# A transformer block on one core: the attention mask moved into a spare row of keys and queries, and a written-out head and end of the first phase

## The reference, cut to what matters

```python
x = x + L0_xattn(layernorm(x), ctx_768, mask)       # 64 sequences x 128 tokens x 256, 16 heads of 16
x = x + L0_ffn(layernorm(x))                        # top-1 routing to 8 experts, capacity 512 rows each
x = x + L1_xattn(layernorm(x), ctx_768)
x = x + L1_ffn(layernorm(x))                        # six nodes of attention with 8 heads

def L0_xattn(x, context, context_mask, ...):
    q, k, v = x @ Wq, context @ Wk, context @ Wv
    scores = where(context_mask[:, None, None, :], q k^T * 0.25, -finfo.max)
    return softmax(scores) v @ Wo

def L0_ffn(x):
    probs = softmax(x @ w_switch + b_switch); route = probs.argmax(-1)
    slot = route * capacity + running count of the route, or none beyond the capacity
    buf = zeros.at[slot].set(x); y = relu(buf w1 + b1) w2 + b2, per expert
```

## Time and profile before

| what | value |
|---|---|
| time, median of 3 runs | 4100.9 us (4100.56 to 4101.86) |
| the profiled execution's own time | 4101.14 us |
| its span in the trace | 4099.0 us |
| granted TensorE clock, mean | 0.99 |
| busy: PE, DVE, ACT, POOL | 98%, 58%, 64%, 47% of the span |
| first phase | 0 to about 660 us |
| expert phase | about 660 to 899 us |
| second layer | 899 us to the end |

### The profile page before, as it was taken

The page is one execution under the profiler, slowest core; times in us unless marked ns, Lnnn a source line. Parts: engine busy times, 40 slices in busy tenths (PEclk is TensorE's granted clock), DMA queues, the critical chain, the costliest instruction groups (busy, mean ns, idle before and its releaser), DMA issues.

```text
span 4099.0 us, 100758 instructions
## 1 busy us (share of the span) xinstructions
PE 4001.1 (98%) x38276; PEld 3406.3 (83%) x38276; DVE 2391.6 (58%) x6184; ACT 2622.6 (64%) x11786; POOL 1930.3 (47%) x2011
## 2 busy tenths in 40 slices
PE   8999998999999999999999999999999999999997
PEld 6888886668888888888888888888888888888886
DVE  5777772016556566666666666666665565666553
ACT  6888881115666666666666666666666666666664
POOL 5888883013444444444444444444444444444443
PEclk9999999999999999999999999999999999999999
DMA  3232214421000000000000000000000000000000
GB/s 104 70 96 72 65 53 135 155 95 40 14 12 14 17 14 14 13 14 14 15 15 13 14 13 13 15 18 12 13 12 12 12 12 12 12 12 12 7 4 9
DMA packets 117866, 129.73 MB, mean 32 GB/s; under 512 B 12006, under 2 KB 110676, under 8 KB 117264
## 3 DMA queue, kind: packets, MB, share of 16 engines
q1 hardware_dynamic: 105648, 109.80, 8.4%
q0 software_dynamic: 6144, 8.43, 0.7%
q10 hardware_dynamic: 5600, 5.07, 0.4%
HBM read 89.68 MB, written 41.94 MB: 32 GB/s over the span
## 4 chain that ended last, share of the span: by engine, by line
PE 76%; DVE 1%; ACT 0%; issue 0%; POOL 0%; POOLq 0%; ACTq 0%
PE c_product L1422 37%; PE c_product L1433 15%; PE c_product L1481 10%; PE c_scores L1471 7%; PE c_product L1504 5%; PE c_product L1492 2%; DVE c_qT L1277 1%; PE c_product L1410 1%; ACT c_probs L1234 0%; PE c_product L1541 0%; ACT c_front_probs L1234 0%; DVE c_nodes L1277 0%; DVE c_neg_max L1286 0%; POOL c_probs L1188 0%; DVE c_nodes L1348 0%
## 5 line engine op out<-in xcount | busy, mean ns | idle before, releaser
L1188 POOL TENSOR_TENSOR c_probs<-c_probs,c_row_inv 128x512 f32<-128x512 f32 x768 | 794.9, 1043 | 1390.4 <-DVE c_row_inv L1289 1384.4
L1234 ACT ACTIVATE c_probs<-c_scores,c_neg_max 128x128 f32<-128x128 f32 x3072 | 1084.3, 407 | 354.1 <-DVE c_neg_max L1286 354.0
L1422 PE MATMUL c_product<-c_nodes,cell_w 128*128 128x256 f32 x4352 | 1067.0, 383 | 4.9 <-DVE c_nodes L1277 3.1
L1422 PEld LDWEIGHTS c_product<-c_nodes,cell_w 128*128 128x128 f32 x4352 | 795.8, 190 | 125.1 <-DVE c_nodes L1277 11.9
L1234 ACT ACTIVATION_READ_ACCUMULATOR c_probs<-c_scores,c_neg_max 128x1 f32 x3072 | 758.5, 247 | 0.0
L1286 DVE TENSOR_REDUCE c_neg_max<-c_scores 128x4 f32<-128x512 f32 x1024 | 658.2, 679 | 169.5 <-PE c_scores L1471 161.7
L1240 ACT COPY c_probsT<-c_product 128x512 f32<-128x512 f32 x768 | 419.8, 600 | 462.2 <-PE c_product L1481 458.2
L1234 ACT ACTIVATE c_front_probs<-c_scores,c_neg_max 128x128 f32<-128x128 f32 x1024 | 364.7, 394 | 170.2 <-DVE c_neg_max L1286 170.2
L1433 PE MATMUL c_product<-cell_w,c_nodes 128*128 128x256 f32 x1792 | 430.1, 380 | 0.0
L445 ACT ACTIVATE a_probs<-a_scores,a_neg_max 128x128 f32<-128x128 f32 x1024 | 361.2, 399 | 84.0 <-DVE a_neg_max L501 83.3
L1481 PE MATMUL c_product<-consts_sb,c_probs 128*128 128x128 f32 x3072 | 404.0, 275 | 5.4 <-POOL c_probs L1188 5.4
(11 more groups left out here) (167 smaller groups left out, 6501.6 us busy)
## 6 DMA issues: line engine op xcount, KB each, us to landing
e_w<-in_L_ffn_w SPq DMA_DIRECT2D x12, 1024.0 KB, 6.1
a_x<-in_x SPq DMA_DIRECT2D x32, 256.0 KB, 2.9
a_ctxT<-in_ctx_pairsT SPq DMA_DIRECT2D x32, 256.0 KB, 3.1
x<-a_x SPq DMA_DIRECT2D x32, 256.0 KB, 2.1
xn<-a_xn SPq DMA_DIRECT2D x32, 256.0 KB, 2.2
c_routed<-xn SPq DMA_DIRECT2D x32, 256.0 KB, 2.7
c_x<-x SPq DMA_DIRECT2D x32, 256.0 KB, 3.1
c_ctxT<-in_ctx_pairsT SPq DMA_DIRECT2D x32, 256.0 KB, 2.8
```

The lines of the kernel that those rows point to most:

```text
L1188: nc.gpsimd.tensor_tensor(e, e, rinv[:, i, r].unsqueeze(2).broadcast_to([P, 4, T]), ALU.mult).then_inc(norm_made, 1)
L1234: a = nc.scalar.activation(probs(n)[:, r, k], S[r][:, k], ACT.Exp, bias=nmax[:, i, r, k:k + 1], accum_out=rsum[:, i, r, k:k + 1])
L1422: i = T_.matmul(m[:, u], w[:, k, u * P:(u + 1) * P], src[:, k], start=n == 0, stop=n == last)
```

## The change

1. The mask is no longer added by a matmul. A head has 16 of the 32 rows that a matmul of queries and keys reads, and the other 16 were zeros on the keys' side. Now `mk` makes two rows-with-mask tiles for two jobs (`MASK_JOBS` = 2), `K^` adds them to the two key copies in a fused instruction, and `Q^` makes two copies of the queries with a 1 in the spare row. Each round has four matmuls per bank and not five, and the wait for the exponentials of the round before stands ahead of the first of them.
2. The first iterations follow written-out lists (`FIRST_PE_HEAD` and so on, put first by `headed`) and the last ones a list too (`FIRST_PE_TAIL`, `FIRST_DVE_TAIL`, by `ended`). From `Tn:0` on PE to the last jobs the order is as it was, apart from `mk`.
3. The 16 zero transfers go behind the loads of jobs 4 to 7, four each. `load(1)` stands ahead of the load of Wo.
4. The first expert's rows are loaded at the end of the first phase, by SP after its wait for all scatters; POOL's wait for them is gone. The tile is that of `kT_even`.
5. ACT runs one small exponential before its list.

```diff
-    MASK_JOBS, SENDS, RING = 4, 3, 3
+    MASK_JOBS, SENDS, RING = 2, 3, 3
...
+            load(1)
             sp.dma_start(wo[:], halves(io["L0_xattn_Wo"])).then_inc(wo_in, 16)
-            load(1)
+            mask_rows(1)
             sp.wait_ge(zero_made, 1)
-            for n in range(parts.shape[0]):
-                sp.dma_start(parts[n], zero).then_inc(buf_zeroed, 16)
-            mask_rows(1)
             for j in range(2, JOBS):
                 load(j)
+                if ZERO_FIRST <= j < ZERO_FIRST + ZERO_LOADS:
+                    n = parts.shape[0] // ZERO_LOADS
+                    for part in range(n * (j - ZERO_FIRST), n * (j - ZERO_FIRST + 1)):
+                        sp.dma_start(parts[part], zero).then_inc(buf_zeroed, 16)
...
             store(JOBS - 1)
+            for p in range(SENDS):
+                sp.wait_ge(sent[p], 16 * PAIR * len(range(p, JOBS, SENDS)))
+            sp.dma_start(first["rows"], halves(buf[0:CAP])).then_inc(first["rows_in"], 16)
...
-            for p in range(SENDS):
-                pool.wait_ge(sent[p], 16 * PAIR * len(range(p, JOBS, SENDS)))
...
+            nc.scalar.activation(e[:, 0], cst[:, C_IOTA:C_IOTA + E], ACT.Exp)
...
-                    V.tensor_scalar(mkb[:, g % 2], mku[:, g % 2], 1.0, NEG, ALU.subtract, ALU.mult).then_inc(mask_made, 1)
+                    for h in range(2):
+                        spare = cst[:, C_SPARE + 3 * h:C_SPARE + 3 * h + 1]
+                        k = V.tensor_scalar(mkr[:, g % 2, h], mku[:, g % 2], spare, spare, ALU.mult, ALU.subtract)
...
-                    V.tensor_scalar(qT[:, o], product(n, j), 0.25, None, ALU.mult).then_inc(prod_used, 1)
+                    for h, q in enumerate((qE, qO)):
+                        c = C_SPARE + 3 * h + 1
+                        k = V.tensor_scalar(q[:, o], m, cst[:, c:c + 1], cst[:, c + 1:c + 2], ALU.mult, ALU.add)
...
-                    V.tensor_scalar(kE[:, o], m, cst[:, C_EVEN:C_EVEN + 1], None, ALU.mult)
-                    V.tensor_scalar(kO[:, o], m, cst[:, C_ODD:C_ODD + 1], None, ALU.mult).then_inc(prod_used, 1)
+                    for h, (a, c) in enumerate(((kE, C_EVEN), (kO, C_ODD))):
+                        k = V.scalar_tensor_tensor(out=a[:, o], in0=m, scalar=cst[:, c:c + 1], op0=ALU.mult, op1=ALU.add,
+                                                   in1=mkr[:, j // MASK_JOBS % 2, h, t0:t0 + W2].unsqueeze(1).broadcast_to([P, 2, W2]))
...
-                        T_.matmul(S[r][:], one_row[g],
-                                  mkb[g, j // MASK_JOBS % 2, off:off + T].unsqueeze(1).broadcast_to([32, 4, T]),
-                                  start=True, stop=False)
-                            i = T_.matmul(S[r][:, k], qT[g, o, u, b * T:(b + 1) * T], w[g, o, u, b * T:(b + 1) * T],
-                                          start=False, stop=k == 3)
+                            i = T_.matmul(S[r][:, k], q[g, o, u, b * T:(b + 1) * T], w[g, o, u, b * T:(b + 1) * T],
+                                          start=True, stop=True)
```

More of the change, by code:

```diff
@@ L43, in consts_array @@
              np.full((P, 2), 1e-5), np.full((P, 2), 1e-6)]
+    for row in (16, 0):
+        spare = (i % 32 == row)[:, None]
+        parts += [spare * NEG, ~spare * 0.25, spare]
     return np.concatenate([np.asarray(a, np.float32) for a in parts], 1)
-C_ID, C_TRI, C_ONE, C_EVEN, C_ODD, C_IOTA, C_HALF, C_EPS5, C_EPS6, C_END = \
-    0, 128, 256, 384, 385, 386, 394, 396, 398, 400
+C_ID, C_TRI, C_ONE, C_EVEN, C_ODD, C_IOTA, C_HALF, C_EPS5, C_EPS6, C_SPARE, C_END = \
+    0, 128, 256, 384, 385, 386, 394, 396, 398, 400, 406
 BANKS = 4
@@ L96, in unfold, with ended @@
     return [(name, k - s) for k in range(min(first, 0), jobs + last) for name, s in order if 0 <= k - s < jobs]
-def with_fused(order, table, job_of, at):
-    order = list(order)
-    for line in table.strip().splitlines():
-        behind, *pieces = line.split()
-        name, k = behind.split(":")
-        i = 0 if name == "start" else order.index((name, job_of(int(k)))) + 1
-        order[i:i] = [(p, at) for p in pieces]
-    return order
+def ended(table, order, jobs):
+    tail = [(t.rpartition(":")[0], jobs - int(t.rpartition(":")[2])) for t in table.split()]
+    return [x for x in order if x not in tail] + tail
 def headed(table, order):
@@ L162, with phase_first_layer @@
 OUT_OF_BOUNDS = 65536.0
-def phase_first_layer(nc, io, scratch, keep, cst, consts_in, cell, w1_first):
+def phase_first_layer(nc, io, scratch, keep, cst, consts_in, cell, first):
     x, ctx, mask, buf = io["x"], io["ctx_pairsT"], io["mask_BxS2_bf1"], scratch["buf"]
@@ L195, in phase_first_layer @@
                                       (FIRST_PE_ORDER, FIRST_DVE_ORDER, FIRST_ACT_ORDER, FIRST_POOL_ORDER))
-    on_pe = with_fused(on_pe, FUSE_PE_PLACES, lambda back: JOBS - 1 - back, JOBS - 1)
-    on_dve = with_fused(on_dve, FUSE_DVE_PLACES, lambda back: JOBS - 1 - back, JOBS - 1)
+    on_pe, on_dve, on_act, on_pool = (headed(head, order) for head, order in (
+        (FIRST_PE_HEAD, on_pe), (FIRST_DVE_HEAD, on_dve), (FIRST_ACT_HEAD, on_act), (FIRST_POOL_HEAD, on_pool)))
+    on_pe, on_dve = ended(FIRST_PE_TAIL, on_pe, JOBS), ended(FIRST_DVE_TAIL, on_dve, JOBS)
     def is_turn(n):
@@ L352, in _ @@
                 if j == 16:
-                    sp.dma_start(w1_first[:], halves(io["L0_ffn_w1"][0])).then_inc(w1_in, 16)
+                    sp.dma_start(first["w1"], halves(io["L0_ffn_w1"][0])).then_inc(w1_in, 16)
                 if j >= X_RING - 1:
@@ L469, in statistics @@
             def statistics(src, i, j):
+                if j >= 1:
+                    dve.wait_ge(var_made[i], j)
                 for b in range(PAIR):
@@ L550, in _ @@
                                     bsw[:].unsqueeze(1).broadcast_to([P, PAIR, E]), ALU.add).then_inc(prod_used, 1)
+                elif n == "gate":
+                    gate = keep["gate"][:, 0:B]
+                    chain(V.reciprocal(gate, pm[:]))
+                    V.tensor_tensor(gate, gate, pm[:], ALU.mult)
                 elif n[0:2] == "r.":
@@ L593, in _ @@
                     raise ValueError(n)
-            gate = keep["gate"][:, 0:B]
-            chain(V.reciprocal(gate, pm[:]))
-            V.tensor_tensor(gate, gate, pm[:], ALU.mult)
         @block.tensor
@@ L741, in _, with phase_experts @@
                     raise ValueError(n)
-def phase_experts(nc, io, scratch, cst, cell, w1_first, early):
+def phase_experts(nc, io, scratch, cst, cell, first, early):
     w1, w2 = io["L0_ffn_w1"], io["L0_ffn_w2"]
@@ L762, in sem @@
             return es.enter_context(nc.semaphore("e_" + name))
-        w1t = [w1_first, sb("w1", [2, H])]
+        w1t = [first["w1"], sb("w1", [2, H])]
         w2t = sb("w2", [2, HC, D])
         b1t, b2t = sb("b1", [E, HC]), sb("b2", [E, D])
-        xr, xT = sb("rows", [2, NR, D]), sb("rowsT", [2, 2, CAP])
+        xr, xT = [first["rows"], sb("rows", [NR, D])], sb("rowsT", [2, 2, CAP])
         hT = sb("hidden", [HC, CAP])
@@ L772, in phase_experts @@
         Y = [es.enter_context(nc.psum_tensor(f"e_out{r}", [P, 2, D], F32)) for r in range(YB)]
-        rows_in, w1_in, w2_in = ([sem(f"{n}{s}") for s in range(2)] for n in ("rows_in", "w1_in", "w2_in"))
+        w1_in, w2_in = ([sem(f"{n}{s}") for s in range(2)] for n in ("w1_in", "w2_in"))
+        rows_in = [first["rows_in"], sem("rows_in1")]
         b1_in, b2_in = sem("b1_in"), sem("b2_in")
```

93 lines of the change are left out of this document (54 added, 39 removed).

## The result

The changed kernel takes **4090.8 us** (median of 20 executions, 4085.4 to 4102.3) beside 4100.8 us (4098.3 to 4106.4) of the kernel before: the ratio of the means is 0.998, 95% interval 0.9974 to 0.9987, that is 5.3 to 10.7 us less, middle 8.2; the medians lie 10.0 us apart. I had forecast 16.7 us less. So the time lies inside the range that I gave (4075 to 4093), and the gain is about half of the forecast one. The profiled execution of the changed kernel took 4085.37 us, the least of the 20, so its trace alone would have told a better story than the median does; three more executions were therefore profiled.

A forecast was written before the change was run, and what follows sets the result against it. In the first phase a ring through PE, DVE and POOL was taken as the bound, with PE and POOL nearly full. Head -10, middle +2.3, end -9 gave -16.7 us from 4101.14: 4084 us, range 4075 to 4093.

The forecast's parts named there:

- the ring through PE, DVE and POOL: First phase: PE's transposes to logits, DVE's statistics, POOL's `rs` and back set the period of 17.79 us.
- the 3.3 us for the waits behind the first exponential: Head: POOL's 3.15 us wait at `rs` of job 4 and similar earlier waits go; 3.3 us won, the loosest estimate.
- the sum of the middle: 27 iterations of the first phase: 14 x (-0.21) + 7 x 0.78 + 6 x (-0.05) = +2.3 us.
- the second layer at nothing: Second layer: instruction order unchanged except where the first expert's rows are loaded, so nothing can come from there.
- Head, forecast -10: Start: first exponential at 19.0 instead of 25.65 us (-6.7), plus 3.3 us of waits; bounds -5 and -13.
- An iteration with a new `mk`: Middle, j = 5, 9, ..., 29: two `mk` add 1.0 us, the shorter ring takes 0.22: +0.78 us each, seven times.
- A plain one: Middle, no `mk` or routing group: without the mask's matmuls 0.21 us less per iteration, then POOL is full.
- The iteration with a routing group: Middle: the new `mk` pair replaces the old one of 0.83 us, +0.17 - 0.22, so -0.05 us each, six times.
- End, forecast -9: Seam: last puts end at 647.6, rows' load lies beside the barrier, PE's experts start about 655; bounds -4 and -13.
- Rival 1: Middle: one of each `mk` pair blocked by a POOL instruction, or `Q^` overruns its cover; +10 us, 4094; chance 0.14.
- Rival 3: Middle: PE falls to its lower clock behind new waits in seven `mk` iterations; costs 37 us, 4121; chance 0.04.
- Rival 2: End: POOL's finish or a product F holds the barrier, only 4 us won; 4089; chance 0.09.

The follow-up runs named there:

- old_head: The changed kernel without its four written-out head lists; 4097.3 us, +3.6 over the unchanged changed kernel on the same chip.
- experiment 2: Asked whether `mk` is the price in the middle, by two variants of the changed kernel: mk_moved 4084.0 us and old_mask 4084.3 us.
- mk_moved: The changed kernel with the two `mk` moved on DVE ahead of S0.x0, out of the ring; 4084.0 us, ratio 0.9955.
- old_mask: The changed kernel with the mask's part alone undone, so a mask matmul again heads each round; 4084.3 us, ratio 0.9958.

## Why the prediction was wrong in size

The direction was right, and so were the ring through PE, DVE and POOL and the gains of head and end. The size was 16.7 us, measured 8.2 (8.9 between the means of the profiles). Three steps failed: the 3.3 us for the waits behind the first exponential, the sum of the middle, and the second layer at nothing. By the means of the profiles:

- **Head, forecast -10, measured -7.65.** The first exponential was counted at 19.0 us and came at 17.2 to 19.5, mean 17.9, a lead of 7.45. What failed is the step "I take 3.3 us" for the waits behind it: the lead at `rs:5` is 7.65, so 0.2 of the 3.3 were left. `rs` of job 4 did lose its 3.15 us of wait and started 12.4 us earlier in the first profile, but from there to `rs` of job 5 it was 21.6 us and not 17.8, since POOL waited 6.2 us on the way instead of 3.1. And old_head is 5.6 us later at the first exponential and 5.7 at `rs:5`: what the lists give is there at the first exponential, where the forecast had counted the new order once already.
- **Middle, forecast +2.3, measured +4.7, of which the work is +9.1 and the clock -4.4.** By the table of experiment 2 four iterations cost 1.36 us more with the clock high, and I had 0.31. An iteration with a new `mk` lost 1.03, not 0.78: `mk` takes 1.11 us of the ring, not 1.0, and a round without the mask is 0.11 us shorter, not 0.22. A plain one won 0.09, not 0.21, for the same reason: the price of the mask was read between two starts, not over the whole round. The iteration with a routing group lost 0.19 where I had a gain of 0.05, and the one behind it lost 0.23 where I had a gain of 0.21; this last loss stays when `mk` is moved (19.70), and its cause was not separated. PE's waits for DVE's copy of the turned rows (11 of 8.4 us in all instead of 5 of 3.6) come from `mk` too, which stands ahead of that copy: in mk_moved they are 6 of 1.7. That the middle came out only 2.4 us beside the forecast is luck: the three low stretches fewer were in no term.
- **End, forecast -9, measured -8.4** (-6.45 and -1.9), 10.7 in the first profile. The forecast's times are those of the kernel before; the first profile's have to be moved by the 3.9 us that it was ahead at `rs:30`. Then its last put ends at 649.0 (forecast 647.6), and the experts start at 656.2 (forecast 655). The mechanism held. But the -1.9 lie behind the start of the experts, and 1.4 of them are the first expert's matmuls at less of the lower clock (16.3 us before, 14.0 to 15.9 now), which was no term of the forecast.
- **Second layer, forecast 0, measured +2.4.** Nothing was changed there but the time at which it starts. One of four profiles lost 6.4 us in its first 63 us. In the last 70 us two have 20.4 us at the lower clock and two 14.8, and end 3 us apart; the two of before have 17.8 and stand between them. This is a term I did not have at all. That the shift of some 10 us moves the work against the low stretches of the clock is my reading and was not tested.

The sum of the four gaps, 2.35 + 2.4 + 0.6 + 2.4, is 7.8 us, the whole miss of 16.7 against 8.9. Rival 1 came true in size, since the work of the middle grew by 9 us where it had 10, though by neither of its two causes: between 165 and 600 us each `mk` instruction took 0.53 to 0.75 us, so none was held up for a multiplication, and PE had no wait for `Q^`. Rival 3 came the other way round: the middle ran at 1.00 instead of 0.98. Rival 2 did not happen.

## What to carry to other kernels

A new instruction is priced by where it stands. The same `mk` costs 1.1 us each time between two steps of the ring, and 0.3 at twice its duration where its engine has slack; before a change is judged, try its instructions in the gaps. An instruction that is taken away is priced over the whole group it stood in (1.22 to 1.11 us here), not from its start to the next. Compare stretches at the same granted clock before a difference is put down to the work: here the clock hid half of what the middle lost. A wait that a new order takes away at one job is only won when the jobs behind it start earlier too. Follow the lead over three or four jobs before it goes into a sum. And a profile is one execution: look where it stands among the timed ones before reading gains of some microseconds out of it, and profile twice.

## What the runs showed of the hardware that I had not expected

- One program, and four profiles whose granted clock is low at different times: 13.7 us at the start of the second layer in one of four (6.4 us lost), the first expert 14.0 us in two and 15.7 and 15.9 in the others. The kernel before gave twice the same places.
- The same wait of PE, 1.8 us, was followed by the lower clock four times from `rs:5` to `rs:30` in the kernel before (two profiles) and in old_mask, and once in the changed kernel (four profiles).
- The x of job 1 was there for DVE between 9.1 and 9.8 us over the four profiles of the changed kernel, with the same issues ahead of it.
- `mk` (128x512 bytes to bf16 on DVE): 0.61 us with POOL waiting, 1.23 us beside POOL's multiplications.
